# Nine products x*Wr per layer moved behind the last segment sum, the weight split parted, Wr loaded from ScalarE's queue

## The reference, cut to what matters

```python
x0 = layernorm(x)
for l in range(3):                      # SAGE layers
    msg = x[src]                        # 20000 x 512, src and dst sorted by dst
    agg = segment_sum(msg, dst, 10000)
    agg = agg / max(deg, 1)
    out = agg @ Wl + bl + x @ Wr
    x = where(out >= 0, out, a * out)
x = x_in + x
x = x + moe(layernorm(x))               # router, top 2 of 8 experts, 512 -> 64 -> 512
```

## Time and profile before

| what | value |
|---|---|
| median of three runs | 2820.04 us |
| the profiled execution | 2825.41 us, span 2824.0 us |
| TensorE busy | 2657.2 us, 94% |
| VectorE busy | 1817.0 us, 64% |
| ScalarE busy | 1254.6 us, 44% |
| GpSimd busy | 1028.4 us, 36% |
| mean DMA | 158 GB/s |

### The profile page before, as it was taken

How to read it: one execution, slowest core, us unless ns; L and a number is a source line. 1 busy time by engine, 2 the same in 40 slices (tenths; PEclk the granted TensorE clock), 3 DMA queues, 4 the chain that set the end, 5 groups by cost and what they waited for, 6 DMA issues and landing times.

```text
span 2824.0 us, 42297 instructions
## 1 busy us (share of the span) xinstructions
PE 2657.2 (94%) x9195; PEld 1494.9 (53%) x9195; DVE 1817.0 (64%) x5090; ACT 1254.6 (44%) x2681; POOL 1028.4 (36%) x1054
## 2 busy tenths in 40 slices
PE   7999999999599999999599999999959999999999
PEld 3444444444388854444278864444425555555554
DVE  5555555555599945555489965555547777777775
ACT  2222244444388844444288864454412222222222
POOL 2222244444244434444333324454422222222221
PEclk9999999999699999999799999999979999999999
DMA  4444377777355557777445547777732222222221
GB/s 134 132 131 133 117 221 232 223 228 228 104 165 165 165 183 224 228 234 227 156 149 164 164 153 226 231 228 224 224 115 87 81 89 83 84 89 79 89 85 50
DMA packets 200918, 446.37 MB, mean 158 GB/s; under 512 B 34383, under 2 KB 34695, under 8 KB 200836
## 3 DMA queue, kind: packets, MB, share of 16 engines
q0 software_dynamic: 64928, 207.55, 26.6%
q1 hardware_dynamic: 135908, 237.66, 23.6%
HBM read 238.50 MB, written 207.11 MB: 158 GB/s over the span
## 4 chain that ended last, share of the span: by engine, by line
PE 70%; DMA 16%; issue 6%; POOL 3%; ACT 2%; DVE 2%; SPq 0%; ACTq 0%; POOLq 0%; DVEq 0%
PE psY L592 20%; DMA rows<-y_rows,lists 14%; PE psY L572 10%; PE psH L572 10%; PE psT L566 5%; PE psY L606 5%; PE psY L614 5%; PE psY L623 5%; POOL rows L500 3%; PE psS L704 3%; PE psM L572 2%; PE psS L705 2%; ACT outs L809 2%; PE psS L566 1%; PE psH L776 1%
## 5 line engine op out<-in xcount | busy, mean ns | idle before, releaser
L592 PE MATMUL psY<-wz,res 128*128 128x512 f32 x1896 | 857.1, 595 | 12.5 <-ACT outs L809 12.5
L500 POOL DMA_INDIRECT rows<-y_rows,lists x471 | 526.9, 1119 | 614.4 <-PE psS L705 468.6
L1141 DVE TENSOR_TENSOR lows<-rows,highs 128x512 fp32r<-128x512 f32 x471 | 326.8, 694 | 508.9 <-ACT highs L809 505.7
L592 PEld LDWEIGHTS psY<-wz,res 128*128 128x128 f32 x1896 | 360.6, 190 | 378.5 <-issue 344.5
L809 ACT ACTIVATE highs<-rows 128x512 fp32r<-128x512 f32 x471 | 296.4, 630 | 582.0 <-DMA rows<-y_rows,lists 579.2
L507 POOL DMA_INDIRECT rows<-sum_rows,nodeI x237 | 293.6, 1239 | 317.2 <-DVE rows L1149 279.3
L481 POOL TENSOR_TENSOR st<-st,small 128x1 f32<-128x1 f32 x158 | 90.0, 570 | 653.4 <-DVE st L1041 653.4
L592 PE MATMUL psY<-wy,res 128*128 128x512 f32 x632 | 286.5, 596 | 0.7 <-ACT res L809 0.7
L572 PE MATMUL psY<-wy,xTs 128*128 128x512 f32 x632 | 287.1, 597 | 0.0
L572 PE MATMUL psH<-wz,hTs 128*128 128x512 f32 x632 | 284.2, 592 | 0.7 <-ACT hTs L809 0.7
L704 PE MATMUL psS<-highs,sel 128*128 128x512 f32 x471 | 249.5, 530 | 36.8 <-ACT outs L809 26.1
(11 more groups left out here) (154 smaller groups left out, 3497.5 us busy)
## 6 DMA issues: line engine op xcount, KB each, us to landing
sum_rows<-outs SPq DMA_DIRECT2D x471, 256.0 KB, 2.8
y_rows<-outs SPq DMA_DIRECT2D x237, 256.0 KB, 2.0
rows<-in_x POOLq DMA_DIRECT2D x78, 256.0 KB, 3.0
outs<-in_x SPq DMA_DIRECT2D x78, 256.0 KB, 2.7
out_rows<-res SPq DMA_DIRECT2D x78, 256.0 KB, 2.1
rows<-y_rows,lists POOLq DMA_INDIRECT x471, 3.8
rows<-sum_rows,nodeI POOLq DMA_INDIRECT x237, 3.5
wy<-in_L_gnn_Wl SPq DMA_DIRECT2D x3, 1024.0 KB, 7.6
```

What stands on the lines that cost most here:

```text
L500: pool.indirect_dma_start(out=rows[:, g, :], out_offset=None, in_=y_d, in_offset=bass.IndirectOffsetOnAxis(ap=col(srcT, t), axis=0), bound ...
L592: mm = pe.matmul(dest, part(t, c), w[:, c, :], start=(c == 0), stop=(c == C - 1))
L1141: dve.tensor_tensor(lows[:, g, :], rows[:, g, :], highs[:, g, :].bitcast(F32), ALU.subtract)\
```

## The change

- `FIRST, LATE = 3, 9`. Three products stand ahead of the first block. `sum_blocks` gives the next 67 products evenly to the 79 blocks of two edge tiles (12 blocks have none); `late_nodes` are the last nine. TensorE does two of them before the mending matmuls and seven behind.
- The products of layers 2 and 3 write to `psH` and `psM` instead of `psY`, and TensorE waits for the last y evictions in layer 1 only.
- SyncE loads the next Wl (or W1) after the first 32 sum stores of the layer, and its sum stores are written out one by one. Its y stores are no longer parted: all follow each other.
- ScalarE issues the load of Wr and of the bias, after the last widening and ahead of the last two y evictions.
- The split is parted in three: `split_high` (8 instructions, before the mending adds), `split_cross` (8, after them), `split_low` (4, after the last product is taken). The first low part stands in `w_part`, which lies where `outs` is, so `split_high` waits for all sum stores.
- VectorE's loop over the blocks is written out, with a product taken behind the edge tiles of its block.

```diff
+FIRST, LATE = 3, 9
+        def psZ(l, s):
+            return (psY[s] if l == 0 else (psH, psM)[s])[:, :]
+        def sum_blocks():
+            due = FIRST
+            for b in range(NT):
+                upto = FIRST + (b + 1) * (NT - FIRST - LATE) // NT
+                nodes = [(t // 2, t % 2) for t in range(due, upto)]
+                due = upto
+                yield nodes, [(t // 4, t % 4) for t in (2 * b, 2 * b + 1) if t < ET]
+        def late_nodes():
+            return [(t // 2, t % 2) for t in range(NT - LATE, NT)]
...
 # SyncE
-                each_four(sp, lambda i, c: store_seg(i, c, l), l == 0)
+                store_segs(l, 0, 32)
+                if l + 1 < LAYERS:
+                    sp.wait_ge(y_ps[0], (l + 1) * uses(0))
+                    sp.wait_ge(y_ps[1], (l + 1) * uses(1))
+                    load_w(wy, Wl[l + 1], wy_in)
+                else:
+                    for e in range(X):
+                        sp.dma_start(wy[:, :, e * F:(e + 1) * F], W1[e].rearrange("(c p) f -> p c f", p=P))\
+                          .then_inc(wy_in, 16)
+                store_segs(l, 32, ET)
...
-                    for i in turns(sp, PAIRS - 1, True):
-                        for c in range(2):
-                            store_y(i, c, l + 1)
-                    sp.wait_ge(ll_ps, (l + 1) * NT)
-                    load_w(wz, Wr[l + 1], wz_in)
-                    all_turns(sp, xd_set, l + 1)
-                    load_row(bvec, bl[l + 1], bvec_in)
-                    store_y(PAIRS - 1, 0, l + 1)
-                    store_y(PAIRS - 1, 1, l + 1)
-                    store_y(PAIRS, 0, l + 1)
+                    each_pair(sp, lambda i, c: store_y(i, c, l + 1), True)
...
 # TensorE
-                pe.wait_ge(parts_set, k)
+                pe.wait_ge(high_parts, k)
...
+                    if first:
+                        pe.wait_ge(low_parts, k)
                     y_low(i, c, k)
...
-                all_turns(pe, y_sb, l + 1)
+                if l == 0:
+                    all_turns(pe, y_sb, l + 1)
...
-                for node, edges in edge_blocks(pe):
-                    z_product(*node, l)
+                for t in range(1, FIRST):
+                    z_product(t // 2, t % 2, l)
+                for nodes, edges in sum_blocks():
+                    for node in nodes:
+                        z_product(*node, l)
                     for e in edges:
                         segment_sum(*e, l)
+                late = late_nodes()
+                for node in late[:2]:
+                    z_product(*node, l)
...
+                for node in late[2:]:
+                    z_product(*node, l)
...
 # ScalarE
+            def load_z(l):
+                act.dma_start(wz[:, :, :], Wr[l].rearrange("(c p) n -> p c n", p=P)).then_inc(wz_in, 16)
+                all_turns(act, xd_set, l)
+                act.dma_start(bvec[:, :], bl[l].partition_broadcast(P)).then_inc(bvec_in, 16)
...
                             widen(i, c, l)
+                            load_z(l)
...
 # VectorE, after the blocks
+                late = late_nodes()
+                take_z(*late[0], l)
                 if l + 1 < LAYERS:
-                    split_w(l)
+                    split_high(l)
+                take_z(*late[1], l)
...  (the two mending adds)
+                take_z(*late[2], l)
+                if l + 1 < LAYERS:
+                    split_cross()
+                for node in late[3:]:
+                    take_z(*node, l)
+                if l + 1 < LAYERS:
+                    split_low(l)
```

More of the change, by code:

```diff
@@ L133, in build @@
         w_low = nc.alloc_sbuf_tensor_at("w_low", [P, C, D], F32R, offset=wz_at)
+        w_part = nc.alloc_sbuf_tensor_at("w_part", [P, C, D], F32R, offset=outs_at)
         w_cross = nc.alloc_sbuf_tensor_at("w_cross", [P, C, D], F32R, offset=hw_at)
@@ L182, in build @@
         acol_in = sem("acol_in")
-        parts_set = sem("parts_set")
+        high_parts = sem("high_parts")
+        low_parts = sem("low_parts")
         xh_set = sem("xh_set")
@@ L387, in store_seg, with store_segs @@
                 sp.dma_start(s_d[rows_of(t)], outs[:, g, :]).then_inc(seg_st[g], 16)
+            def store_segs(l, first, last):
+                for t in range(first, last):
+                    store_seg(t // 4, t % 4, l)
             for l in range(LAYERS):
-                each_four(sp, lambda i, c: store_seg(i, c, l), l == 0)
+                store_segs(l, 0, 32)
[8 more added lines that the diff above has]
+                store_segs(l, 32, ET)
                 starts_d = s_d[0:ET * P].rearrange("(t p) d -> t p d", p=P)[:, 0, :]
@@ L398, in _ @@
                     sp.dma_start(rows[0:r, START_SLOT[b], :], starts_d[b * P:b * P + r]).then_inc(mend_in[b], 16)
-                if l + 1 < LAYERS:
-                    load_w(wy, Wl[l + 1], wy_in)
-                else:
+                if l + 1 == LAYERS:
                     for g in range(4):
@@ L407, in _ @@
                     sp.dma_start(b2s[:, :].bitcast(F32), b2_d).then_inc(b2_back, 16)
-                    for e in range(X):
-                        sp.dma_start(wy[:, :, e * F:(e + 1) * F], W1[e].rearrange("(c p) f -> p c f", p=P))\
-                          .then_inc(wy_in, 16)
                 if l + 1 == LAYERS:
@@ L693, in z_product @@
                 pe.wait_ge(z_sb[s], l * uses(s) + n)
-                kept_product(psY[s][:, :], t, wz, z_ps[s])
+                kept_product(psZ(l, s), t, wz, z_ps[s])
             def segment_sum(i, c, l):
@@ L1129, in take_z @@
                 dve.wait_ge(z_ps[s], l * uses(s) + n + 1)
-                dve.tensor_tensor(kept(t), psY[s][:, :], bvec[:, :], ALU.add).then_inc(z_sb[s], 1)
+                dve.tensor_tensor(kept(t), psZ(l, s), bvec[:, :], ALU.add).then_inc(z_sb[s], 1)
             def select(i, c, l):
@@ L1178, in split_x, with each_row, row, split_high @@
                    .then_inc(xd_set[s], 1)
-            def split_w(l):
-                all_turns(dve, z_ps, l + 1)
+            def each_row(ins):
+                for q in range(C):
+                    ins(q).then_inc(vchain, 1)
+                done[0] += C
+                dve.wait_ge(vchain, done[0])
+            def row(buf, q):
+                return buf[:, q, :].bitcast(F32)
+            def split_high(l):
                 for g in range(4):
                     dve.wait_ge(seg_ps[g], (l + 1) * uses(g))
+                    dve.wait_ge(seg_st[g], 16 * (l + 1) * uses(g))
                 dve.wait_ge(wy_in, 16 * (l + 2))
[L1187 to L1194, removed]
                 each_row(lambda q: dve.tensor_scalar(w_cross[:, q, :], wy[:, q, :], UNDER, None, ALU.mult))
-                each_row(lambda q: dve.tensor_tensor(w_low[:, q, :], wy[:, q, :], row(w_cross, q), ALU.subtract))
-                each_row(lambda q: dve.tensor_tensor(w_high[:, q, :], wy[:, q, :], row(w_low, q), ALU.subtract))
+                each_row(lambda q: dve.tensor_tensor(w_part[:, q, :], wy[:, q, :], row(w_cross, q), ALU.subtract))
+            def split_cross():
+                each_row(lambda q: dve.tensor_tensor(w_high[:, q, :], wy[:, q, :], row(w_part, q), ALU.subtract))
+                dve.sem_inc(high_parts, 1)
                 each_row(lambda q: dve.scalar_tensor_tensor(w_cross[:, q, :], row(w_cross, q), -1.0 / STEP,
-                                                            row(w_low, q), ALU.mult, ALU.add))
-                each_row(lambda q: dve.tensor_scalar(w_low[:, q, :], row(w_low, q), STEP, None, ALU.mult))
-                dve.sem_inc(parts_set, 1)
+                                                            row(w_part, q), ALU.mult, ALU.add))
+            def split_low(l):
+                all_turns(dve, z_ps, l + 1)
+                each_row(lambda q: dve.tensor_scalar(w_low[:, q, :], row(w_part, q), STEP, None, ALU.mult))
+                dve.sem_inc(low_parts, 1)
             for l in range(LAYERS):
@@ L1211, in take_edge @@
                     low(*e, l)
[L1213 to L1218, removed]
                 take_z(0, 0, l)
+                take_z(0, 1, l)
                 take_edge((0, 0))
                 take_edge((0, 1))
-                for node, edges in edge_blocks(dve):
-                    block_of(node, edges)
+                for t in range(2, FIRST):
+                    take_z(t // 2, t % 2, l)
+                for nodes, edges in sum_blocks():
+                    for e in two_on(edges):
+                        take_edge(e)
+                    for node in nodes:
+                        take_z(*node, l)
+                late = late_nodes()
+                take_z(*late[0], l)
                 if l + 1 < LAYERS:
-                    split_w(l)
+                    split_high(l)
+                take_z(*late[1], l)
                 for b, r in BLOCKS:
```

## The result

| | median of the runs | profiled execution | span |
|---|---|---|---|
| before | 2820.34 us (2816.15 to 2822.12, 4 runs) | 2825.41 us | 2824.0 us |
| after | 2864.51 us (2857.24 to 2876.64, 4 runs) | 2871.64 us | 2870.0 us |

The ratio is 1.0163, 95% interval 1.0119 to 1.0208. Forecast were 2841 us and 2808 to 2860. The direction was right, the size half of what came.

The account below looks back on a forecast made before the run. The prediction took the phase to be paced largely by a ring of gathers, not by PE. Its terms, 9.1 - 12 + 10 + 14 = +21 us, gave 2841 us as a median, range 2808 to 2860.

Parts of the forecast that it names:

- What bounds the phase: Sum phase: many turns wait for the ring of four edge tiles (9.08 us), not PE's own work (8.70 us).
- R1: Rival, faster: the sum phase yields when products leave it; 2812 us, down to 2780 if every turn quickens; chance 0.17.
- (b): Products taken out of the sum phase: in ring-bound turns this moves nothing; -4 us a phase, -12 in all.
- the ring: Sum phase: four edge tiles cycle through sum, gather, landing and copy; 9.08 us a turn, PE with 0.38 us to spare.
- (c): Weight loads moved inside the sum phase cost late landings: +3 us twice, +4 in layer 3, +10 in all.
- (a): Start of the phase: first sum later by +2.3 us in layer 1, +3.4 each in layers 2 and 3; +9.1 in all.
- (d): Gap from last sum to next x: nine products lengthen it by +2.6, +2.4 and +8.9 us; +14 in all.
- PE itself is late next: Gap: PE's nine products, instead of split and mending, become what is late, overshooting by 14 us.
- the price of the mending chain alone: Gap: with the split out of the way, the next x could start +23.3 us after the last sum.
- R4: Rival, worse: loads hold the ring, (c) is +20 and (b) nothing; +43, 2863 us; chance 0.10.
- What would show it: Signs if right: phases 352 to 360 us, long turns near the 16th block, unbroken PE run, gaps of 37 to 38 us.

Follow-up runs that it names:

- e6: The kernel before the change, with 11 products x*Wr a layer cut to one matmul of 8 columns, their results left out: 2852.98 us, ratio to before 1.0101.
- e3: The changed kernel, with the loads of the next Wl and of W1 put back behind the mending loads: 2872.06 us, ratio to before 1.019.
- e7: The kernel before the change, with only the loads of the next Wl and of W1 moved behind the 32nd sum store: 2802.28 us, ratio 0.9923.
- e1: The changed kernel, with a whole unsignalled product computed in each of the 12 blocks a layer that have none: 2853.06 us, ratio to before 1.0107.
- e8: The kernel before the change, with the next Wl in four spaced loads of 256 KB and W1's eight loads spaced out: 2796.45 us, ratio 0.9893.

## Why the prediction was wrong, by its own steps

- *What bounds the phase*: right. No kernel had a phase below 353 us, whatever work PE was relieved of, and relief made it longer. R1 (a bound PE) is refuted by the products left out.
- *(b) "In a ring-bound turn this frees PE and moves nothing ... I take -4 a phase"*: this is the step that failed. It treated a freed PE as harmless. Left out alone, the products cost 22.9 us of phase (e6). Moved, with no load in the phase, they cost 19.1, of which 2.4 are the later last sums by the forecast's 0.8 each (e3). So by these traces the -12 should have been between +17 and +23. It also counted twelve empty blocks a phase where eleven can leave a hole. The hole's length could be read ahead: a product of 3.43 us and the ring's 0.38 us of slack is 3.8 us (measured 3.9 at most, 2.7 in the mean), and the earlier trace rows show what PE does after an idle time (two products in 8.69 us instead of 6.9). I wrote "partly slow, after its idle time" there and did not put it to the empty blocks. The Trainium skill has the rule: TensorE: Matmul & The Clock Gate, HAM oscillation — how this bites in real kernels, says that an engine that waits between its groups of matmuls falls back to the low clock each time and pays again. The rows of e6 and of the kernel after agree at the places shown: 3.26 and 3.81 us idle, then 5.21 and 5.29 us. They do not agree on "each time": behind 10 of the 33 holes the product took 4.2 us or less; a hole of 2.87 us was followed by a product of 3.60 us, one of 1.35 us by one of 4.51.
- *(c)* was +10 and measured +7.3 by e7 and 6.6 as the difference of the changed kernel and e3, both no larger than the scatter of this sum; how it costs was not foreseen whole, since the product behind the late landing is slow too.
- *(a)* +9.1: measured +10.2 (4.8, 3.4, 2.0). In layer 2 Wr landed 7.3 us after its issue, between the two ends that were taken, 6.1 and 9.0. In layer 1 PE idled 1.87 us before the third product, which then took 5.40 us.
- *(d)* +14 with the 0.8 of the last sum: from the last sum +11.4 expected and +11.7 measured. "PE itself is late next" held, and so did the price of the mending chain alone: +23.3 forecast, 23.5 and 23.8 in e7.
- R4 came nearest in time (2863 us), but by another cause: it laid all to the loads, and e3, without them in the phase, has the same time.
- *What would show it*: phases "at 352 to 360 us" was wrong, the long turn near the 16th block, the full PE run in the gap and its 37 to 38 us were right.

What stays open: after which holes the clock falls and after which it does not, and why the times of the changed kernel spread over 19 us (2857 to 2877) where the kernel before spreads over 6 beside it. No run was made for either.

## What to carry to other kernels

An engine at 97% can still be the filler of a latency-bound ring. Work taken out of such a ring brings nothing, and on TensorE it can cost: here behind two holes in three, of 1.3 to 3.9 us, the next product ran in part at the low clock, and the ring waited for it. To shorten a gap, first take out of its chain what need not be in it (here the split, or the load it waits for: 8 to 12 us a layer), and only then ask what could fill it; filling it with more work than the chain is long (31 us against 24) lengthens it. And a big load beside a latency-bound ring is better tried in pieces.

## What the runs showed that I had not expected

113 us less TensorE work made a kernel 28.6 us slower (e6), and 36 wasted products made another 11.4 us faster (e1). A load of 1 MB in one piece made intervals of up to 9.1 us between two pairs of sums (e7); in pieces it left none over 6.9, and the phases as before (358.6 us in the mean before, 359.0 in e8).
